# First layer of an equivariant GNN kernel: the dependent half of a chunk is run one chunk later, heads two later and last

## The chip, the cores and the metric

The kernel runs on one core of one Trainium2 chip. The metric is the device time of one execution in microseconds (us), the median of three runs. Nothing is shared with other cores, so there is one span, one TensorE clock and one set of 16 DMA engines to watch.

## The reference, cut to what matters

Two message-passing layers over 3125 nodes and 100000 edges. Each node has 64 scalars and 32 vectors of 3 components. The change touches only the edge loop of the first layer, an attention layer. For every edge that loop computes:

```python
msg = (s_n @ W_src)[src] + (s_n @ W_dst)[dst]          # gathered rows of two node tables, added
w1 = rbf @ W_rbf                                       # edge factors
m1_s, m1_v = _cg_tp(msg_s, msg_v, y0, y1, w1[...])     # products of features, factors and y
a = leaky_relu(m1_s @ W_alpha) * alpha_dot             # attention logits
val_s = m1_s @ Ws_val
val_v = einsum(m1_v, Wv_val) * sigmoid(val_s @ Wg)     # gated values
m2_s, m2_v = _cg_tp(sigmoid(val_s), val_v, y0, y1, w2)
hs, hv = m2_s @ Ws_vlin, einsum(m2_v, Wv_vlin)         # the heads' values, stored per edge
```

## The kernel before, in words

The edges are cut into 392 chunks of 256 (two groups of 128 partitions, G = 2). A chunk passes through five engines in a chain:

- GpSimd (POOL) gathers the rows of `src_tab` and `dst_tab` by four indirect DMAs, six chunks ahead.
- TensorE (PE) makes the factors W1 (`factors0`, L792), ScalarE (ACT) weighs them (`weigh0`, L1111 to L1115).
- VectorE (DVE) adds the gathered rows (`joined0`, L1481) and builds the first mixed tensor M (`products0` to `rest_of_v0`, L1506 to L1532, semaphore `m`).
- PE transposes M (`t1`, L800), ACT copies it out (`copies`, L1126, semaphore `c1`), and PE multiplies it (`e1`, L822 and L824) into the edge bank E1, which holds logits, gates and values.
- DVE takes E1: logits `la` (`gated`, L1543), `svy` (`gated_up`, L1549), `vals` (`summed`, L1556). ACT takes the sigmoids (`squash`, L1137 and L1138, semaphore `sg`). DVE makes V2 (`scaled`, L1574) and the second mixed tensor M2 (`mixed_dots`, `mixed_rest`, L1587 to L1600, semaphore `tp`), ACT its other blocks (`weigh2`, L1149 and L1154, semaphore `m2a`).
- PE transposes M2 (`t2`, also L800), ACT copies it (L1126 again, semaphore `c2`), PE makes the heads in the bank HP (`hm`, L847 and L849, semaphore `h`).
- DVE forms tG and the vector heads (`head_products`, L1610, and `head_values`, L1619, semaphore `hv`), ACT the scalar heads (`scalars0`, L1164, semaphore `hs`), and SP stores the rows (`store`, L507).

Nothing but the code sets the order. Each engine has one in-order list of functions, `stage0(t, total)`, called once for each step t; the number added to t says which chunk the function works on in that step. `loop_steps` writes out the first and last steps and runs the others in a hardware loop of 8 steps, so the loop's branch (L338) comes once in 8 chunks, 47 times in all. Between engines there are only semaphores. Within DVE a second instruction that needs the first one's result waits on DVE's own semaphore `s_dve` (`ch.wait`). `ch.restart` (L81) clears that semaphore at the start of each step.

PE and DVE share three tight resources: E1 has one buffer, HP has one buffer, and M and M2 have two each. A wait such as `pe.wait_ge(LA["hv"], v.num)` in `hm` says that the heads of the chunk before must have been read from HP.

Of the kernel before, what the change touches and what calls it, by code (L numbers as in the profile page):

```python
# [8 lines left out]
ALU = mybir.AluOpType  # L9
# [3 lines left out]
P = 128  # L13
# [4 lines left out]
G = 2  # L18
# [5 lines left out]
C = 32  # L24
# [9 lines left out]
Q = 4  # L34
# [116 lines left out]
def program(nc, a, out):  # L151
    ctx = ExitStack()
    with ctx:
# [6 lines left out]
        def sem(name):  # L160
            return ctx.enter_context(nc.semaphore(name))
# [169 lines left out]
        def loop_steps(eng, q, sups, wide, lead, tail, stage):  # L331


            total = sups * q
            for t in range(-lead, 2 * q):
                stage(Step(t, None, wide, q), total)
            end = sups - 2 - sups % 2
            with eng.Fori(2, end, 2) as base:  # L338
                for u in range(2 * q):
                    stage(Step(u, base, wide, q), None)  # L340
            for t in range(end * q, total + tail):
                stage(Step(t, None, wide, q), total)
# [16 lines left out]
        def inside(v, total):  # L359
# [2 lines left out]

        LA = dict(ix=[sem(f"a_ix{u}") for u in range(2)], rb=[sem(f"a_rb{u}") for u in range(2)],
                  ga=[sem(f"a_ga{u}") for u in range(8)], st=[sem(f"a_st{u}") for u in range(4)],
                  **{k: sem(f"a_{k}") for k in ("w", "ws", "m", "t1", "c1", "e1", "bent", "sg", "vg", "m2a", "tp", "t2", "c2",
                                                "h", "hs", "hv")})

        LM = {k: sem(f"m_{k}") for k in ("ld", "cp", "ab", "mx", "all", "tab", "ix", "ga", "got")}
# [17 lines left out]
        def _(sp):  # L386
# [103 lines left out]
            def load_rbf(v, total):  # L490

                if v.place or not inside(v, total):
                    return
                if v.sup_past(2):
                    sp.wait_ge(LA["w"], v.num - Q)
                sp.dma_start(rbf[0:16, v.sslot].rearrange("f q g p -> f (q g p)"),
                             a["rbf_line"][:, bass.ds(v.data(), 1), :].rearrange("f a e -> f (a e)"))\
                    .then_inc(LA["rb"][v.sslot], 16)

            def store(v, total):  # L500

                if not inside(v, total):
                    return
                sp.wait_ge(LA["hv"], v.num + 1)
                sp.wait_ge(LA["hs"], v.num + 1)
                row = h_tab.ap()[bass.ds(v.column(0), 1), :]
                sp.dma_start(bass.AP(row.tensor, row.offset, [[NC * D, P], [1, G * D]]),  # L507
                             hst[:, v.slot].rearrange("p g f -> p (g f)")).then_inc(LA["st"][v.slot], 16)

            def sp0(t, total):  # L510
                load_places(t + 8, total)
                load_rbf(t + 5, total)
                store(t + -2, total)
            loop_steps(sp, Q, NS, False, 8, 2, sp0)

            def fill(table, width):
                zero = bass.AP(zeros.tensor, zeros.offset, [list(zeros.ap[0]), [0, AR // P], [1, width]])
# [222 lines left out]
        def _(pe):  # L740
# [42 lines left out]
            def factors0(v, total):  # L783

                if not inside(v, total):
                    return
                if v.place == 0:
                    pe.wait_ge(LA["rb"][v.sslot], v.sup_round(16))
                if v.past(1):
                    pe.wait_ge(LA["ws"], v.num)  # L790
                for g in range(G):
                    ins = nc.tensor.matmul(W1[:, 224 * g:224 * (g + 1)], rbf[:, v.sslot, v.place, g, :], w_rbf[:, :],  # L792
                                           start=True, stop=True)
                ins.then_inc(LA["w"], 1)
# [17 lines left out]
            def e1(v, total):  # L812

                if not inside(v, total):
                    return
                pe.wait_ge(LA["c1"], v.num + 1)
                if v.past(1):

                    pe.wait_ge(LA["vg"], v.num)
                    pe.wait_ge(LA["sg"], v.num)  # L820
                for g in range(G):
                    nc.tensor.matmul(E1[:, 0, ES * g:ES * (g + 1)], MT[:, 0, g, :], w_ms0[:, :], start=True, stop=True)  # L822
                    for b in range(2):
                        ins = nc.tensor.matmul(E1[:, 1, P * g:P * (g + 1)], MT[:, 1 + b, g, :], w_mv0[:, b, :],  # L824
                                               start=(b == 0), stop=(b == 1))
                ins.then_inc(LA["e1"], 1)

            def t2(v, total):
                if not inside(v, total):
                    return  # L830

                pe.wait_ge(LA["m2a"], v.num + 1)
                pe.wait_ge(LA["tp"], v.num + 1)
                if v.past(1):
                    pe.wait_ge(LA["c2"], v.num)
                turn(M2[:, v.par], TR2, LA["t2"])
# [15 lines left out]

            def stage0(t, total):
                e1(t + -1, total)
                t2(t + -2, total)
                t1(t, total)
                factors0(t + 2, total)
                hm(t + -2, total)
            loop_steps(pe, Q, NS, False, 2, 2, stage0)

            pe.wait_ge(s_flag, 1)
            general = pe.value_load(flag[0:1, 0:1], min_val=0, max_val=EP)
# [176 lines left out]
        def _(act):  # L1039
# [79 lines left out]
            def copies(v, total, turned, tr, dst, sem_done, freed):  # L1119
                if not inside(v, total):  # L1120
                    return
                act.wait_ge(LA[turned], v.num + 1)

                if v.past(1):
                    act.wait_ge(LA[freed], v.num)
                nc.scalar.activation(dst[:, 0:3].rearrange("p k g e -> p (k g e)"),  # L1126
                                     tr[:, 0:3 * G, :].rearrange("p a e -> p (a e)"), ACT.Copy).then_inc(LA[sem_done], 1)
# [29 lines left out]
            def scalars0(v, total):  # L1157

                if not inside(v, total):
                    return  # L1160
                act.wait_ge(LA["hv"], v.num + 1)
                if v.past(4):
                    act.wait_ge(LA["st"][v.slot], v.slot_round(16, 4) - 16)
                nc.scalar.activation(hst[:, v.slot, :, 0:S], ax(HP[:, 0:1], (S, G), (1, S)), ACT.Copy).then_inc(LA["hs"], 1)  # L1164

            def stage0(t, total):
                weigh0(t + 1, total, 1)
                squash(t + -1, total)
                copies(t + -2, total, "t2", TR2, MT2, "c2", "h")
                copies(t, total, "t1", TR1, MT, "c1", "e1")  # L1170
                weigh2(t + -1, total)
                weigh0(t + 2, total, 0)
                scalars0(t + -2, total)
            loop_steps(act, Q, NS, False, 2, 2, stage0)

            act.wait_ge(s_flag, 1)
            general = act.value_load(flag[0:1, 0:1], min_val=0, max_val=EP)
# [172 lines left out]
        def _(dve):  # L1350
# [201 lines left out]
            def summed(v, total, up):  # L1552

                if inside(v, total):
                    ch.wait(up)
                    return ch.count(TT(vals[:, :, :, :], ax(E1[:, 1, 0:1], (P, G), (C, 3), (1, C)), svy[:, :, :, :], ALU.add))  # L1556

            def bent_sums(v, total):

# [3 lines left out]
                ch.count(nc.vector.tensor_reduce(alog[:, bass.ds(v.column(0), G), :].rearrange("p c h -> p (c h)"),  # L1563
                                                 ax(la[:, 0, 0:1], (LG, G * H), (1, LG)), AX.X, ALU.add))

            def scaled(v, total, summed):

                if not inside(v, total):
                    return
                dve.wait_ge(LA["sg"], v.num + 1)  # L1570
                if v.past(1):
                    dve.wait_ge(LA["m2a"], v.num)
                ch.wait(summed)
                TT(k3(V2[:, :, :]), ax(gate[:, v.par, 0, 0:1], (C, G), (0, 3), (1, C)), vals[:, :, :, :], ALU.mult)\  # L1574
                    .then_inc(LA["vg"], 1)

# [26 lines left out]
            def head_products(v, total):  # L1603

                if not inside(v, total):
                    return
                dve.wait_ge(LA["h"], v.num + 1)
                if v.past(1):
                    dve.wait_ge(LA["hv"], v.num)
                return ch.count(TT(k3(tG[:, :, :]), ax(HP[:, P + 96:P + 97], (P, G), (0, 3), (1, C)), y_of(v, 1, (1, 3), (0, C)), ALU.mult))  # L1610
# [9 lines left out]

            def stage0(t, total):
                ch.restart()
                gated(t + -1, total)
                joined = joined0(t + 1, total)
                ups = gated_up(t + -1, total)
                parts = products0(t + 1, total, joined)
                done = summed(t + -1, total, ups)
                scaled(t + -1, total, done)
                crossed0(t + 1, total, parts)
                dots = mixed_dots(t + -1, total)  # L1630
                bent_sums(t + -1, total)
                mixed_rest(t + -1, total, dots)
                up = head_products(t + -2, total)
                crosses = others0(t + 1, total, parts)
                rest_of_s0(t + 1, total, parts)
                head_values(t + -2, total, up)
                rest_of_v0(t + 1, total, parts, crosses)
            loop_steps(dve, Q, NS, False, 1, 2, stage0)
            ch.restart()


# [314 lines left out]
```

## Time and profile before

| | |
|---|---|
| median of 3 runs | 3868.43 us (3867.98 to 3871.22) |
| the profiled execution, first to last instruction | 4838.8 us |
| edge loop of the first layer | about 85 to 3043 us of that span |
| edge loop of the second layer | about 3448 to 4779 us |
| mean granted TensorE clock | 0.917 of full speed |

The profiled execution is a separate one, and the only time of its own that is known is its span, 970.4 us above the median of the runs. An engine is busy while one of its instructions runs, overlap counted once. "Idle before" an instruction is put down to the semaphore that arrived last; "remote" means that the profile shows no instruction that sent it at that moment. The starts of matmuls are recorded and their ends modelled.

### The profile page before, as it was taken

The numbers are of one execution on the slowest core, as the hardware profiler recorded it, in microseconds if no ns is written. First come the engines' busy times: TensorE is split into PE (matmuls) and PEld (weight loads), VectorE is DVE, ScalarE is ACT, GpSimd is POOL, SyncE is SP. The second block draws the span as 40 slices with busy tenths as digits, with TensorE's granted clock in tenths as the row PEclk, the third lists the DMA queues.
The fourth block names the chain that finished last, engine by engine and source line by source line (L and its number), as shares of the span: only waits on it lengthen the run. The fifth ranks groups of instructions, "written<-read, shape, count | busy, mean of one in ns | idle before, by whom it ended". The sixth has DMA issues, their size and how long they took to land. (4 is left out here: it accounts for less than half of the span.)

```text
span 4838.8 us, 96593 instructions
## 1 busy us (share of the span) xinstructions
PE 3739.1 (77%) x21340; PEld 2828.7 (58%) x21340; DVE 3611.5 (75%) x12738; ACT 3088.6 (64%) x11217; POOL 2474.0 (51%) x2474
## 2 busy tenths in 40 slices
PE   3677777777777777777777778597788888888887
PEld 3676766666676767766666667487433333333334
DVE  4677777777777777777777778788677877777875
ACT  3566666666666666666666667475666666666664
POOL 3445555555555545555555454011366666666663
PEclk7899999999999999999999999799899998998998
DMA  3222222222222222222222222798233333333333
GB/s 101 64 64 68 72 67 68 67 70 67 66 71 72 67 63 72 68 72 67 66 68 68 64 71 63 228 274 226 60 77 77 77 79 76 79 78 77 81 78 103
DMA packets 296922, 411.02 MB, mean 85 GB/s; under 512 B 98580, under 2 KB 231572, under 8 KB 296596
## 3 DMA queue, kind: packets, MB, share of 16 engines
q0 software_dynamic: 127568, 211.04, 19.0%
q1 hardware_dynamic: 169284, 199.21, 12.7%
q8 instruction: 24, 0.39, 0.0%
q14 instruction: 46, 0.38, 0.0%
HBM read 309.09 MB, written 100.94 MB: 85 GB/s over the span
## 5 line engine op out<-in xcount | busy, mean ns | idle before, releaser
L654 POOL DMA_INDIRECT ACC<-src_tab,idx x784 | 777.2, 991 | 1184.8 <-DVE M L1532 852.2
L721 POOL DMA_INDIRECT ACC<-hid_tab,idx x784 | 828.7, 1057 | 453.6 <-issue 250.7
L800 PE MATMUL TR<-ident,M 128*128 128x128 f32 x4704 | 682.7, 285 | 472.0 <-DVE M L1532 380.3
L654 POOL DMA_INDIRECT TAB<-dst_tab,idx x784 | 767.9, 980 | 261.2 <-issue 260.9
L800 PEld LDWEIGHTS TR<-ident,M 128*128 128x128 f32 x4704 | 549.0, 146 | 554.6 <-DVE M L1532 440.0
L1126 ACT ACTIVATE MT<-TR 128x768 f32<-128x768 f32 x784 | 609.5, 842 | 158.2 <-remote 135.7
L1164 ACT ACTIVATE ACC<-HP 128x128 f32<-128x128 f32 x392 | 109.2, 279 | 750.8 <-DVE ACC L1619 625.8
L1115 ACT ACTIVATE ACC<-W,ACC 128x64 f32<-128x64 f32 x2352 | 587.9, 348 | 0.0
L849 PE MATMUL HP<-w_hv,MT 128*128 128x128 f32 x3136 | 564.4, 306 | 0.0
L1309 ACT ACTIVATE ACC<-TR,y 128x128 f32<-128x128 f32 (+1 forms) x1568 | 421.9, 455 | 208.6 <-remote 100.3
L1610 DVE TENSOR_TENSOR tG<-HP,ACC 128x192 f32<-128x192 f32 x392 | 140.1, 357 | 523.1 <-remote 331.3
L824 PE MATMUL E<-w_mv,MT 128*128 128x128 f32 x3136 | 508.3, 288 | 0.0
L824 PEld LDWEIGHTS E<-w_mv,MT 128*128 128x128 f32 x3136 | 471.8, 204 | 0.0
L849 PEld LDWEIGHTS HP<-w_hv,MT 128*128 128x128 f32 x3136 | 453.9, 208 | 0.0
L999 PE MATMUL HP<-M,ohE 128*128 128x480 f32 x800 | 407.9, 636 | 48.8 <-DVE M L1863 29.3
L822 PE MATMUL E<-w_ms,MT 128*128 128x168 f32 x1568 | 383.0, 328 | 68.2 <-ACT MT L1126 62.9
L847 PE MATMUL HP<-w_hs,MT 128*128 128x64 f32 x1568 | 315.0, 286 | 153.4 <-ACT MT L1126 120.5
L999 PE MATMUL E<-M,ohE 128*128 128x480 f32 x768 | 396.6, 643 | 42.5 <-issue 23.3
L792 PE MATMUL W<-w_rbf,rbf 128*128 128x224 f32 x1568 | 405.7, 384 | 27.2 <-DMA rbf<-in_rbf_line 13.8
L847 PEld LDWEIGHTS HP<-w_hs,MT 128*128 128x128 f32 x1568 | 267.1, 208 | 259.3 <-ACT MT L1126 178.7
L1309 ACT ACTIVATE TAB<-TR,y 128x128 f32<-128x128 f32 (+1 forms) x1568 | 415.7, 430 | 0.5 <-PE TR L984 0.5
L984 PEld LDWEIGHTS TR<-w_edge,ACC 64*128 64x128 f32 x1568 | 126.3, 197 | 441.0 <-issue 196.3
(279 smaller groups left out, 8063.1 us busy)
## 6 DMA issues: line engine op xcount, KB each, us to landing
h_tab<-ACC SPq DMA_DIRECT2D x392, 160.0 KB
SC<-h_tab SPq DMA_DIRECT2D x50, 640.0 KB, 4.9
TAB<-h_tab SPq DMA_DIRECT2D x48, 640.0 KB, 5.1
ACC<-in_e64T SPq DMA_DIRECT2D x98, 256.0 KB
ACC<-src_tab,idx POOLq DMA_INDIRECT x784
TAB<-dst_tab,idx POOLq DMA_INDIRECT x784
ACC<-hid_tab,idx POOLq DMA_INDIRECT x784
agg_tab<-ACC POOLq DMA_DIRECT2D x49, 240.0 KB
```

Of the source, the lines that this page charges most:

```text
L654: pool.indirect_dma_start(tile[:, v.slot8, g, :], None, table.ap(), bass.IndirectOffsetOnAxis(ap=idx[:, v.sslot, c:c + 1], axis=0))\
L721: pool.indirect_dma_start(gat1[:, v.slot8, g, :], None, hid_tab.ap(), bass.IndirectOffsetOnAxis(ap=idx[:, v.sslot, c:c + 1], axis=0))\
L792: ins = nc.tensor.matmul(W1[:, 224 * g:224 * (g + 1)], rbf[:, v.sslot, v.place, g, :], w_rbf[:, :], start=True, stop=True)
L800: ins = nc.tensor.transpose(to[:, b * G + g, :], Mt[:, g, lo:lo + w], ident[:, :])
L822: nc.tensor.matmul(E1[:, 0, ES * g:ES * (g + 1)], MT[:, 0, g, :], w_ms0[:, :], start=True, stop=True)
L824: ins = nc.tensor.matmul(E1[:, 1, P * g:P * (g + 1)], MT[:, 1 + b, g, :], w_mv0[:, b, :], start=(b == 0), stop=(b == 1))
L847: nc.tensor.matmul(HP[:, S * g:S * (g + 1)], MT2[:, 0, g, :], w_hs0[:, :], start=True, stop=True)
L849: ins = nc.tensor.matmul(HP[:, P + P * g:P + P * (g + 1)], MT2[:, 1 + b, g, :], w_hv0[:, b, :], start=(b == 0), stop=(b == 1))
L999: ins = nc.tensor.matmul(AG[v.sslot][:, 0:MW], ohE[:, v.slot, g, :], M[:, v.par, g, :], start=(v.place == 0 and g == 0), stop=(v.place == ...
L1115: ins = nc.scalar.activation(o[:, 160 + 64 * k:224 + 64 * k], w[:, 160:224], ACT.Copy, scale=y_at(v, g, 1 + k))
L1126: nc.scalar.activation(dst[:, 0:3].rearrange("p k g e -> p (k g e)"), tr[:, 0:3 * G, :].rearrange("p a e -> p (a e)"), ACT.Copy).then_inc( ...
L1309: ins = nc.scalar.activation(WS[v.slot][:, g, P * k:P * k + hi - lo], wg_[:, lo:hi], ACT.Copy, scale=y1[:, v.sslot, c:c + 1])
```

## The change

Every function keeps its instructions. What changes is the chunk on which it works in a step, its place in the list, and four waits.

- DVE, ACT: everything from `gated` to `mixed_rest` and `squash`, `weigh2` works on chunk t-2 instead of t-1; the copy of the first transposes moves from t to t-1. `weigh0(…, 1)` does its chunk a step earlier.
- PE: `t2` and `hm` work on t-3 instead of t-2; `e1` and `t1` stay. `factors0` runs one chunk further ahead.
- The heads (`head_products`, `head_values`, `scalars0`, `store`) work on t-4 instead of t-2. On DVE both stand last in the step; on ACT the copy of the second transposes stands last.
- A new semaphore `vs` is raised by `summed`. PE's `e1` waits for `vs` and not for `vg`, so E1 is free once `vals` is made. `scaled` waits for `vs` where it waited for `s_dve`.
- `scalars0` waits for `h`, and `head_products` waits for `hs`; before, `scalars0` waited for `hv` and `head_products` for `h`.

```diff
@@ PE
-                    pe.wait_ge(LA["vg"], v.num)
+                    pe.wait_ge(LA["vs"], v.num)
...
                 e1(t + -1, total)
-                t2(t + -2, total)
+                t2(t + -3, total)
                 t1(t, total)
-                factors0(t + 2, total)
-                hm(t + -2, total)
-            loop_steps(pe, Q, NS, False, 2, 2, stage0)
+                factors0(t + 3, total)
+                hm(t + -3, total)
+            loop_steps(pe, Q, NS, False, 3, 3, stage0)
@@ ACT
-                act.wait_ge(LA["hv"], v.num + 1)
+                act.wait_ge(LA["h"], v.num + 1)
...
-                weigh0(t + 1, total, 1)
-                squash(t + -1, total)
-                copies(t + -2, total, "t2", TR2, MT2, "c2", "h")
-                copies(t, total, "t1", TR1, MT, "c1", "e1")
-                weigh2(t + -1, total)
+                squash(t + -2, total)
+                copies(t + -1, total, "t1", TR1, MT, "c1", "e1")
+                weigh2(t + -2, total)
                 weigh0(t + 2, total, 0)
-                scalars0(t + -2, total)
-            loop_steps(act, Q, NS, False, 2, 2, stage0)
+                scalars0(t + -4, total)
+                weigh0(t + 2, total, 1)
+                copies(t + -3, total, "t2", TR2, MT2, "c2", "h")
+            loop_steps(act, Q, NS, False, 2, 4, stage0)
@@ DVE
-                    return ch.count(TT(vals[:, :, :, :], ax(E1[:, 1, 0:1], (P, G), (C, 3), (1, C)), svy[:, :, :, :], ALU.add))
+                    TT(vals[:, :, :, :], ax(E1[:, 1, 0:1], (P, G), (C, 3), (1, C)), svy[:, :, :, :], ALU.add).then_inc(LA["vs"], 1)
...
-                ch.wait(summed)
+                dve.wait_ge(LA["vs"], v.num + 1)
...
-                dve.wait_ge(LA["h"], v.num + 1)
+                dve.wait_ge(LA["hs"], v.num + 1)
...
-                up = head_products(t + -2, total)
                 crosses = others0(t + 1, total, parts)
                 rest_of_s0(t + 1, total, parts)
-                head_values(t + -2, total, up)
                 rest_of_v0(t + 1, total, parts, crosses)
-            loop_steps(dve, Q, NS, False, 1, 2, stage0)
+                up = head_products(t + -4, total)
+                head_values(t + -4, total, up)
+            loop_steps(dve, Q, NS, False, 1, 4, stage0)
@@ SP
-                load_rbf(t + 5, total)
-                store(t + -2, total)
-            loop_steps(sp, Q, NS, False, 8, 2, sp0)
+                load_rbf(t + 6, total)
+                store(t + -4, total)
+            loop_steps(sp, Q, NS, False, 8, 4, sp0)
```

On DVE, the second half of one step of the written-out first steps, with the semaphores that each instruction waits for (`a_h` is `h`, and so on; shapes are partitions by elements):

```order
 L1600 TENSOR_TENSOR M<-fX 128x2x96 [waits s_dve]
-L1610 TENSOR_TENSOR tG<-HP,ACC 128x192 [waits a_hv,a_h]
 L1517 TENSOR_TENSOR fX<-ACC 128x2x2x32
 L1518 TENSOR_TENSOR fX<-ACC 128x2x64
 L1524 TENSOR_TENSOR M<-M 128x2x32 [waits s_dve]
 L1525 TENSOR_TENSOR M<-ACC 128x2x128
-L1619 TENSOR_TENSOR ACC<-HP,tG 128x2x96 [waits s_dve]
 L1531 TENSOR_TENSOR M<-fX 128x2x96 [waits s_dve]
 L1532 TENSOR_TENSOR M<-ACC 128x2x96
+L1610 TENSOR_TENSOR tG<-HP,ACC 128x192 [waits a_hv,a_hs]
+L1619 TENSOR_TENSOR ACC<-HP,tG 128x2x96 [waits s_dve]
 L81 ISA [waits s_dve]
```

Four instructions stood between tG (L1610) and L1619, which needs it; now none does.

On ACT, one step before the change, from the copy L1164 of the scalar heads:

```order
L1164 ACTIVATE ACC<-HP 128x2x64 [waits a_hv]
L1113 ACTIVATE ACC<-W,ACC 128x96
L1115 ACTIVATE ACC<-W,ACC 128x64 x3
L1137 ACTIVATE gate<-E 128x64 [waits a_vg,a_t2,a_bent]
L1138 ACTIVATE M<-E 128x2x2x32
L1126 ACTIVATE MT<-TR 128x768 [waits a_h,a_t2]
L1126 ACTIVATE MT<-TR 128x768 [waits a_e1,a_t1]
L1149 ACTIVATE M<-M,ACC 128x64 [waits a_sg]
```

and the same stretch of a step after it:

```order
L1164 ACTIVATE ACC<-HP 128x2x64 [waits a_h]
L1113 ACTIVATE ACC<-W,ACC 128x96
L1115 ACTIVATE ACC<-W,ACC 128x64 x3
L1126 ACTIVATE MT<-TR 128x768 [waits a_h,a_t2]
L1137 ACTIVATE gate<-E 128x64 [waits a_vg,a_t2,a_bent]
L1138 ACTIVATE M<-E 128x2x2x32
L1126 ACTIVATE MT<-TR 128x768 [waits a_e1,a_t1]
L1149 ACTIVATE M<-M,ACC 128x64 [waits a_sg]
```

The copy of the second transposes (the first L1126 of each) now comes ahead of the sigmoids, and L1164 no longer waits for DVE's heads.

## Rows read from the trace of the kernel before

**Rows 1.** Page, part 1: busy time by engine, whole span

```profile
PE 3739.1 (77%) x21340; PEld 2828.7 (58%) x21340; DVE 3611.5 (75%) x12738; ACT 3088.6 (64%) x11217; POOL 2474.0 (51%) x2474
```

**Rows 2.** Windows: length, busy PE PEld DVE ACT POOL, PE clock, DMA share, GB/s

```profile
0.00:85.00 85.00, 32.86 (x162) 27.52 (x162) 48.74 (x123) 37.03 (x93) 9.30 (x24) 0.83 0.43 116
85.00:3043.00 2958.00, 2252.81 (x15672) 2041.29 (x15672) 2184.80 (x8623) 1918.74 (x7047) 1540.80 (x1564) 0.93 0.25 68
3043.00:3448.00 405.00, 294.36 (x1894) 270.46 (x1894) 311.47 (x424) 241.66 (x774) 51.11 (x60) 0.88 0.78 223
3448.00:4779.00 1331.00, 1119.21 (x3309) 451.37 (x3310) 1046.67 (x3525) 870.54 (x3248) 871.86 (x827) 0.91 0.32 77
...
2998.00:3037.00 39.00, 35.84 (x272) 32.18 (x272) 37.02 (x150) 31.62 (x115) 0.00 (x0) 1.00 0.10 35
```

**Rows 3.** Groups by line, first layer's loop: busy, mean ns | idle before

```profile
L1574 DVE TENSOR_TENSOR V<-gate,vals 128x192 f32<-128x192 f32 x392 | 140.5, 358 | 52.5 <-DVE vals L1556 0.5
...
L1610 DVE TENSOR_TENSOR tG<-HP,ACC 128x192 f32<-128x192 f32 x392 | 140.1, 357 | 523.1 <-remote 331.3 <-PE HP L849 158.0 <-issue 33.2
...
L1543 DVE SCALAR_TENSOR_TENSOR la<-E,adot 128x144 f32<-128x144 f32 x392 | 119.2, 304 | 179.1 <-remote 143.8 <-PE E L824 34.9
```

**Rows 4.** Timeline, mid-loop: start, length, instruction, idle before

```profile
1509.12 0.31 DVE L1543 SCALAR_TENSOR_TENSOR la<-E,adot 128x144 f32<-128x144 f32 x1
...
1509.79 0.32 ACT L1138 ACTIVATE M<-E 128x128 f32<-128x128 f32 x1
...
1510.30 0.34 DVE L1556 TENSOR_TENSOR vals<-E,svy 128x192 f32<-128x192 f32 x1
1510.78 0.36 DVE L1574 TENSOR_TENSOR V<-gate,vals 128x192 f32<-128x192 f32 x1
...
1511.80 0.66 PE L849 MATMUL HP<-w_hv,MT 128*128 128x128 f32 x4
...
1514.24 0.36 DVE L1610 TENSOR_TENSOR tG<-HP,ACC 128x192 f32<-128x192 f32 x1 [1.35 <-remote]
1514.51 0.28 DVE L1517 TENSOR_TENSOR fX<-ACC 128x128 f32<-128x128 f32 x1
```

**Rows 5.** Timeline: the last gather of the first layer's loop

```profile
2995.83 0.95 POOL L654 DMA_INDIRECT TAB<-dst_tab,idx  x1 [0.30 <-issue]
```

**Rows 6.** Timeline after it: one chunk on DVE and PE

```profile
3003.54 0.30 DVE L1543 SCALAR_TENSOR_TENSOR la<-E,adot 128x144 f32<-128x144 f32 x1
3003.68 0.64 PEld L800 LDWEIGHTS TR<-ident,M 128*128 128x128 f32 x6 [0.45 <-DVE M L1532]
...
3005.28 0.30 PEld L847 LDWEIGHTS HP<-w_hs,MT 128*128 128x128 f32 x2 [0.24 <-ACT MT L1126]
...
3006.22 0.66 PE L849 MATMUL HP<-w_hv,MT 128*128 128x128 f32 x4
...
3006.62 0.30 PEld L822 LDWEIGHTS E<-w_ms,MT 128*128 128x128 f32 x2
...
3007.14 0.35 DVE L1610 TENSOR_TENSOR tG<-HP,ACC 128x192 f32<-128x192 f32 x1
...
3008.08 0.69 PEld L800 LDWEIGHTS TR<-ident,M 128*128 128x128 f32 x6
...
3009.08 0.30 DVE L1543 SCALAR_TENSOR_TENSOR la<-E,adot 128x144 f32<-128x144 f32 x1
```

**Rows 7.** Groups by line on POOL, second layer's loop

```profile
L721 POOL DMA_INDIRECT ACC<-hid_tab,idx x779 | 823.8, 1057 | 448.4 <-issue 245.4 <-DVE M L1863 199.3 <-remote 2.7
L694 POOL DMA_DIRECT2D agg_tab<-ACC x48 | 48.5, 1010 | 4.8 <-issue 4.7
```

**Rows 8.** The loop's branch and the semaphore's clearing on DVE's sequencer

```profile
L338 DVEq ALU_OP  x91: 40/40/40, 238.0 to 4695.7; - x91
L338 DVEq COMPARE_BRANCH  x91: 50/56/72, 238.1 to 4695.8; - x91
...
L81 DVEq EVENT_SEMAPHORE_RANGE_CLEAR  x895: 54/54/55, 57.5 to 4777.2; - x179
```

More of the change, by code:

```diff
@@ L364, in program @@
                   ga=[sem(f"a_ga{u}") for u in range(8)], st=[sem(f"a_st{u}") for u in range(4)],
-                  **{k: sem(f"a_{k}") for k in ("w", "ws", "m", "t1", "c1", "e1", "bent", "sg", "vg", "m2a", "tp", "t2", "c2",
+                  **{k: sem(f"a_{k}") for k in ("w", "ws", "m", "t1", "c1", "e1", "bent", "sg", "vs", "vg", "m2a", "tp", "t2", "c2",
                                                 "h", "hs", "hv")})
@@ L1564, in bent_sums, with scaled @@
                                                  ax(la[:, 0, 0:1], (LG, G * H), (1, LG)), AX.X, ALU.add))
-            def scaled(v, total, summed):
+            def scaled(v, total):
                 if not inside(v, total):
@@ L1622, in stage0 @@
                 ch.restart()
-                gated(t + -1, total)
+                gated(t + -2, total)
                 joined = joined0(t + 1, total)
-                ups = gated_up(t + -1, total)
+                ups = gated_up(t + -2, total)
                 parts = products0(t + 1, total, joined)
-                done = summed(t + -1, total, ups)
-                scaled(t + -1, total, done)
+                summed(t + -2, total, ups)
+                scaled(t + -2, total)
                 crossed0(t + 1, total, parts)
-                dots = mixed_dots(t + -1, total)
-                bent_sums(t + -1, total)
-                mixed_rest(t + -1, total, dots)
-                up = head_products(t + -2, total)
+                dots = mixed_dots(t + -2, total)
+                bent_sums(t + -2, total)
+                mixed_rest(t + -2, total, dots)
                 crosses = others0(t + 1, total, parts)
                 rest_of_s0(t + 1, total, parts)
-                head_values(t + -2, total, up)
                 rest_of_v0(t + 1, total, parts, crosses)
-            loop_steps(dve, Q, NS, False, 1, 2, stage0)
+                up = head_products(t + -4, total)
+                head_values(t + -4, total, up)
+            loop_steps(dve, Q, NS, False, 1, 4, stage0)
             ch.restart()
```

## The prediction

> **What bounds the kernel now.** I read the totals first. In the profiled execution VectorE (DVE) is busy 3611.5 us, and no engine is near its span of 4838.8 us [rows 1]. By stretches, the first layer's edge loop takes 2958 us, 7.55 us for each of its 392 chunks, and DVE is busy 2185 us of them, 5.57 a chunk [rows 2]. Then I asked where DVE is idle in that loop. It is idle 523 us ahead of tG (L1610), which waits for the heads from TensorE (PE); 179 us ahead of `la` (L1543), which waits for the edge bank E1; and 52 us ahead of V2 (L1574) [rows 3]. Read so, the change takes away the dearest wait of the kernel, since the heads that DVE reads will have been made a step earlier.
>
> I don't trust that reading, for two reasons.
>
> First, the timed runs. Their median is 3868 us, and the profile shows DVE busy for 3611 of that. All its idle time in a timed run, in both layers, at the start and at the end, is then 257 us at most (if its instructions take as long there), against 1227 us in the profile. So some 970 us of waiting exist only in the profiled execution, and the question is which.
>
> Second, the waits themselves. In the middle of the loop the last matmul of the heads ends by the profile at 1511.80 + 0.66 = 1512.46, and tG starts at 1514.24, 1.78 us later, released by "remote" [rows 4]. The last gather of this loop is issued at 2995.83 [rows 5]. Behind it the same code runs otherwise: the heads' last matmul ends at 3006.88, and tG starts at 3007.14, straight behind the instruction before it. `la` comes at 3003.54 and again at 3009.08, a step of 5.54 us with no wait [rows 6]. From 2998 to 3037, with POOL silent, DVE is busy 37.0 of 39 us [rows 2]. So the chain of waits through PE does fit under DVE's own work. What stretches a step from 5.54 to 7.55 us is that PE's signals arrive late while gathers run.
>
> How much of that lateness is in the timed runs? In the profile it costs (7.55 - 5.54) x 392 = 786 us. The second layer's loop takes 1331/392 = 3.40 us a chunk [rows 2]. POOL needs there two gathers of 1.06 us, each behind an idle 245.4/779 = 0.31 us, and an eighth of an add of 1.01 + 0.3 us: 2.90 us [rows 7]. If that loop falls to this floor in the timed runs, it gives back 0.50 x 392 = 194 us. 786 + 194 = 980 us, and 970 are missing. So I take it that the timed runs have next to none of the lateness, and that the first loop is bound by DVE there at about 5.6 us a step.
>
> **The change, part by part.**
>
> *The waits for tG, `la` and V2.* The gain is what the first loop still waits in a timed run: call it W. By the sum above it is about -10 us, that is 0. Upper bound: let the second layer fall to DVE's own busy time, 1047 us, a return of 284 us; then 786 + 284 - 970 leaves W = 100 us. Let also the stretch between the loops fall from 405 to DVE's 311 us, and W is 194 us. I take 20 us, near the low end, because POOL's row prices the second layer above DVE's.
>
> *tG and L1619 now stand side by side.* L1619 needs tG and waits for it through `s_dve`. Before, four instructions stood between and hid that. The nearest row is V2 behind `vals`: they start at 1510.30 and 1510.78, 0.48 us apart, with `vals` lasting 0.34, so a dependent pair pays 0.14 us from end to start. ACT's sigmoids (1509.79 + 0.32) were long done, so this wait was for `vals` [rows 4]. tG with a successor that needs nothing starts it 0.27 us later (1514.24 to 1514.51). With the dependent pair it is 0.36 + 0.14 = 0.50. Cost 0.22 us a chunk, 0.22 x 392 = 86 us. It is not hidden by anything, since DVE is in order and is the bound. Bounds: 0 if the sequencer handed over at once, 0.22 by the row.
>
> The Trainium skill (VectorE: DVE Perf Modes, section "The DRAIN you can't avoid") says that a semaphore after each copy cost no more than one after the last: "the semaphore costs nothing extra here". By that rule this term would be 0. This trace does not agree: in the 7.55 us steps as in the 5.54 us steps V2 starts 0.48 us behind `vals`, and independent instructions of this size 0.27 us.
>
> *The branch.* Once in 8 chunks, 47 times, DVE's sequencer must wait for tG before it reaches L1619, and only then does it meet the loop's register operation (0.040), branch (0.056) and the clearing of `s_dve` (0.054) [rows 8], a move and two more register operations, and then `la`. L1619 covers 0.27 us of it. Low bound 0 (0.15 us of listed time is under 0.27); high bound six such instructions at 0.14 us each less 0.27, 0.57 us, or 27 us in all. I take the middle, 14 us.
>
> *`vs` for `vg` and `s_dve`.* The wait of V2 stays as it is with another name. E1 is freed at the end of `vals` (1510.30 + 0.34) and not of V2 (1510.78 + 0.36): 0.50 us earlier for PE. PE's step has slack where it isn't late: it waits 0.45 us for M and 0.24 us for the copy [rows 6]. Worth 0 here.
>
> *The heads' new waits.* PE's `hm` for chunk t-3 waits until L1619 has read HP for chunk t-4, and that is now the last instruction of DVE's step. Behind it in PE's queue stand `e1`, `t2`, `t1` and the factors. `hm` takes 1.34 us (3005.28 to 3006.62), `e1` 1.46 (to 3008.08) [rows 6]. So E1 is filled some 3 us into DVE's next step, and `la` of that chunk comes only at the step after. tG waits for ACT's `scalars0`, about 4 us into the step, and stands 5 us into it. Both fit, and I cost them at 0. If the cover goes (PE at half clock, `hm` and `e1` twice as long), PE's round is late before DVE's.
>
> *SP and POOL.* The store waits for the same two heads; the loads of `rbf` keep their distance to `factors0`, since both moved by one. POOL waits for `m`, which DVE raises 0.77 us before its step's end, as before at the same distance of chunks. 0.
>
> *Filling and draining.* Two more steps at the end, nearly empty: between 0 and two steps of 5.54, I take 5 us.
>
> Sum against the median: 3868 + 86 + 14 + 5 - 20 = 3953 us. Against the profiled execution's own span of 4838.8 us it reads otherwise, since there the lateness is real. The step falls from 7.55 to between 5.8 us (5.54 + 0.22 + 0.04) and some 6.3 us, and the span to 4838.8 - 392 x (1.75 to 1.25) = 4150 to 4350 us. I expect a shorter profile and longer timed runs.
>
> **The rivals.**
>
> *The waits are real and the change pays.* For it: every row of idle time. Against it: 3868 us have no room for more than W = 194 us. With that W the time is 3868 + 105 - 194 = 3779 us. It decides from W = 105 us, 0.27 us a chunk. If instead DVE's instructions were all shorter in the timed runs, in the ratio 3868/4839, the gain would be 1.75 x 392 x 0.8 = 549 us: 3320 us. DVE's step of 5.54 us has nothing in it that a quiet PE shortens, so I give the second little. Together 0.18.
>
> *Nothing moves.* W is near 100 us, or the pair tG and L1619 costs little (the skill's rule: 3868 + 14 + 5 - 20 = 3867 us). 3861 to 3876. 0.12.
>
> *PE becomes the bound.* ACT now copies the second transposes last, PE makes the heads last, and `e1` stands behind them. At half clock that round is 0.87 + 2 x 1.34 + 2 x 1.46 + 0.8 + waits, above 7.3 us. The granted clock in this loop is 0.93 [rows 2]; if such steps are one in ten, 39 x 1.5 = 59 us come on top: 4012 us. 0.05.
>
> **How the numbers follow.** A difference under 0.2% (8 us) can't be told from none here. My case, slower by DVE's own step, has 0.65, with its own range of 3880 to 4000: W from 0 to 95, the branch from 0 to 27, the end from 0 to 12. Slower in all 0.70, same 0.12, faster 0.18. The range to hold the time 8 times in 10 is 3820 to 4005, which leaves out most of the faster cases and the half of PE's.
>
> **What would show it.** In the profile after: no idle time ahead of tG, L1619 starting 0.50 us behind tG with 0.14 us idle before it in each chunk (about 52 us of a new idle row at L1619), and a step of 5.76 us behind the last gather in place of 5.54. The span falls while the median rises. I am wrong if that quiet stretch still shows 5.54, if the median falls, or if `hm` or ACT's last copy has DVE waiting at `la` or V2.

## The result and the profile after

The changed kernel takes 3938.2 us (median of four runs, 3936.6 to 3944.2) where the kernel before takes 3868.2 (3866.7 to 3871.2): a ratio of 1.0182, 95% interval 1.0168 to 1.0197. It is slower by 70 us; 3953 us, 85 more than before, was predicted.

Its profiled execution has a span of 3935.9 us and so stands for the timed runs. That of before does not (4838.8 us), so I profiled the unchanged kernel once more, and after is read beside that second profile of before. Page of the kernel after, span and busy time by engine:

```profile
span 3935.9 us, 96689 instructions
PE 3541.6 (90%) x21340; PEld 2675.8 (68%) x21340; DVE 3583.7 (91%) x12738; ACT 3085.8 (78%) x11217; POOL 2638.3 (67%) x2474
```

Page of before, second profile:

```profile
span 3861.1 us, 96593 instructions
PE 3505.3 (91%) x21340; PEld 2635.6 (68%) x21340; DVE 3558.4 (92%) x12738; ACT 3055.0 (79%) x11217; POOL 2488.1 (64%) x2474
```

The kernel before fits in 3861 us with DVE busy 3558 of them, so the 970 us that the first profile has more, and the idle time in [rows 3] that goes with them, belong to that one execution. Windows of after, the first layer's loop, the stretch between, the second layer's loop (columns as in [rows 2]):

```profile
85.00:2380.00 2295.00, 2146.73 (x15673) 1920.63 (x15672) 2168.30 (x8627) 1929.31 (x7049) 1723.78 (x1564) 1.00 0.32 87
2380.00:2790.00 410.00, 299.57 (x1911) 272.60 (x1912) 315.88 (x448) 242.37 (x781) 59.05 (x66) 0.87 0.77 220
2790.00:3875.00 1085.00, 1021.36 (x3292) 416.19 (x3290) 1029.35 (x3496) 856.50 (x3240) 845.43 (x820) 1.00 0.40 94
```

Windows of before, second profile, the same three stretches:

```profile
85.00:2310.00 2225.00, 2110.52 (x15672) 1879.80 (x15672) 2146.80 (x8629) 1895.98 (x7049) 1575.27 (x1564) 1.00 0.34 91
2310.00:2707.00 397.00, 292.67 (x1894) 270.48 (x1894) 304.28 (x420) 240.01 (x772) 51.40 (x60) 0.88 0.78 223
2707.00:3799.00 1092.00, 1028.39 (x3307) 419.31 (x3308) 1036.76 (x3520) 861.49 (x3248) 851.38 (x827) 1.00 0.39 94
```

The bounds of the stretches are read off by eye, but the place is clear: the first layer's loop is some 70 us longer, and the second layer's is not (1085 against 1092). The granted clock there is 1.00 in both, so TensorE's clock has no part in it. Groups by line of after, first loop:

```profile
L1574 DVE TENSOR_TENSOR V<-gate,vals 128x192 f32<-128x192 f32 x392 | 140.5, 358 | 53.2 <-ACT M L1138 1.2
L1619 DVE TENSOR_TENSOR ACC<-HP,tG 128x192 f32<-128x192 f32 x392 | 140.4, 358 | 40.6
L1610 DVE TENSOR_TENSOR tG<-HP,ACC 128x192 f32<-128x192 f32 x392 | 138.0, 352 | 4.5 <-ACT ACC L1164 4.5
L1506 DVE TENSOR_TENSOR M<-ACC 128x192 f32<-128x192 f32 x392 | 136.9, 349 | 0.5 <-DVE svy L1549 0.2
L1543 DVE SCALAR_TENSOR_TENSOR la<-E,adot 128x144 f32<-128x144 f32 x392 | 117.3, 299 | 18.2 <-DVE tG L1610 17.9
```

The same groups of before, second profile, which take the place of [rows 3]:

```profile
L1574 DVE TENSOR_TENSOR V<-gate,vals 128x192 f32<-128x192 f32 x392 | 140.4, 358 | 52.5 <-DVE vals L1556 0.5
L1506 DVE TENSOR_TENSOR M<-ACC 128x192 f32<-128x192 f32 x392 | 139.2, 355 | 15.1 <-ACT ACC L1115 14.6 <-DVE svy L1549 0.2
L1610 DVE TENSOR_TENSOR tG<-HP,ACC 128x192 f32<-128x192 f32 x392 | 135.8, 346 | 2.9 <-PE HP L849 2.7
L1543 DVE SCALAR_TENSOR_TENSOR la<-E,adot 128x144 f32<-128x144 f32 x392 | 115.9, 296 | 0.7 <-PE E L824 0.6
```

Two idle rows are new, 40.6 us ahead of L1619 and 18.2 ahead of `la`; one is gone, 14.6 us at L1506 for ACT's weighing L1115. The idle times at tG and `la`, 523 and 179 us in [rows 3], were 2.9 and 0.7 us. Timeline of after, two places: at the loop's branch, and the end of a step without the branch:

```profile
644.48 0.35 DVE L1610 TENSOR_TENSOR tG<-HP,ACC 128x192 f32<-128x192 f32 x1
644.94 0.36 DVE L1619 TENSOR_TENSOR ACC<-HP,tG 128x192 f32<-128x192 f32 x1
645.68 0.31 DVE L1543 SCALAR_TENSOR_TENSOR la<-E,adot 128x144 f32<-128x144 f32 x1 [0.39 <-DVE tG L1610]
...
1004.13 0.35 DVE L1532 TENSOR_TENSOR M<-ACC 128x192 f32<-128x192 f32 x1
1004.39 0.35 DVE L1610 TENSOR_TENSOR tG<-HP,ACC 128x192 f32<-128x192 f32 x1
1004.85 0.36 DVE L1619 TENSOR_TENSOR ACC<-HP,tG 128x192 f32<-128x192 f32 x1
1005.13 0.30 DVE L1543 SCALAR_TENSOR_TENSOR la<-E,adot 128x144 f32<-128x144 f32 x1
```

L1619 starts 0.46 us behind tG (mean of all 392 steps). Independent neighbours start 0.26 to 0.28 apart (L1532 to tG, L1619 to `la`). The difference is more than the idle time that the group shows (40.6/392 = 0.10 us): two independent instructions overlap by some 0.08 us, and a dependent pair loses that too. At the branch `la` starts 0.74 us behind L1619 in place of 0.28: 0.46 us, once in 8 chunks.

The longer step is DVE's own and not POOL's. Behind the last gather of the loop, with POOL silent, `la` follows `la` by 5.74 us in after, and by 5.54 us in the second profile of before:

```profile
2334.82 0.30 DVE L1543 SCALAR_TENSOR_TENSOR la<-E,adot 128x144 f32<-128x144 f32 x1
2340.56 0.30 DVE L1543 SCALAR_TENSOR_TENSOR la<-E,adot 128x144 f32<-128x144 f32 x1
...
2263.07 0.30 DVE L1543 SCALAR_TENSOR_TENSOR la<-E,adot 128x144 f32<-128x144 f32 x1
2268.61 0.30 DVE L1543 SCALAR_TENSOR_TENSOR la<-E,adot 128x144 f32<-128x144 f32 x1
```

The row of L1506 holds more than its idle time too. In the kernel before it starts 0.27 us behind `svy` (L1549) in six steps of eight, 0.32 in one, and 0.66 in the step behind the branch; in after it is 0.27 throughout. That makes 21 us in 392 chunks. Timeline of before, second profile:

```profile
674.21 0.35 DVE L1549 TENSOR_TENSOR svy<-E,ACC 128x192 f32<-128x192 f32 x1
674.87 0.36 DVE L1506 TENSOR_TENSOR M<-ACC 128x192 f32<-128x192 f32 x1 [0.31 <-ACT ACC L1115]
```

### The profile page after: what moved, and what is told of

The parts are those of the page before. It is cut to its first block and busy times, and to the rows that moved or that the text cites. A ratio compares the mean times of both kernels' runs of the same rounds, so it can differ in the third digit from the quotient of the medians.

```text
span 3935.9 us, 96689 instructions
## 1 busy us (share of the span) xinstructions
PE 3541.6 (90%) x21340; PEld 2675.8 (68%) x21340; DVE 3583.7 (91%) x12738; ACT 3085.8 (78%) x11217; POOL 2638.3 (67%) x2474
## 5 line engine op out<-in xcount | busy, mean ns | idle before, releaser
L654 POOL DMA_INDIRECT ACC<-src_tab,idx x784 | 852.9, 1088 | 339.9 <-issue 230.2
L654 POOL DMA_INDIRECT TAB<-dst_tab,idx x784 | 874.9, 1116 | 250.1 <-issue 248.5
L1126 ACT ACTIVATE MT<-TR 128x768 f32<-128x768 f32 x784 | 663.4, 846 | 5.2 <-PE TR L800 5.2
L1115 ACT ACTIVATE ACC<-W,ACC 128x64 f32<-128x64 f32 x2352 | 580.1, 339 | 0.0
L800 PE MATMUL TR<-ident,M 128*128 128x128 f32 x4704 | 579.5, 273 | 0.0
L849 PE MATMUL HP<-w_hv,MT 128*128 128x128 f32 x3136 | 520.1, 288 | 0.0
L824 PEld LDWEIGHTS E<-w_mv,MT 128*128 128x128 f32 x3136 | 437.5, 192 | 0.0
L849 PEld LDWEIGHTS HP<-w_hv,MT 128*128 128x128 f32 x3136 | 413.2, 192 | 0.0
L822 PE MATMUL E<-w_ms,MT 128*128 128x168 f32 x1568 | 382.8, 326 | 30.3 <-ACT MT L1126 24.6
L792 PEld LDWEIGHTS W<-w_rbf,rbf 128*128 128x128 f32 x1568 | 267.5, 190 | 185.5 <-ACT ACC L1115 170.3
L999 PE MATMUL E<-M,ohE 128*128 128x480 f32 x768 | 358.6, 590 | 15.5 <-DVE M L1863 14.3
L1154 ACT ACTIVATE M<-V,ACC 128x96 f32<-128x96 f32 x784 | 251.0, 367 | 82.2 <-DVE V L1574 78.0
```

Source lines behind the costliest of these rows:

```text
L654: pool.indirect_dma_start(tile[:, v.slot8, g, :], None, table.ap(), bass.IndirectOffsetOnAxis(ap=idx[:, v.sslot, c:c + 1], axis=0))\
L800: ins = nc.tensor.transpose(to[:, b * G + g, :], Mt[:, g, lo:lo + w], ident[:, :])
L849: ins = nc.tensor.matmul(HP[:, P + P * g:P + P * (g + 1)], MT2[:, 1 + b, g, :], w_hv0[:, b, :], start=(b == 0), stop=(b == 1))
L999: ins = nc.tensor.matmul(AG[v.sslot][:, 0:MW], ohE[:, v.slot, g, :], M[:, v.par, g, :], start=(v.place == 0 and g == 0), stop=(v.place == ...
L1115: ins = nc.scalar.activation(o[:, 160 + 64 * k:224 + 64 * k], w[:, 160:224], ACT.Copy, scale=y_at(v, g, 1 + k))
```

## The experiments

The ratios are against runs of the kernel before, made beside each experiment on the same chip. Their medians are 3862.0 to 3863.6 us; beside after it was 3868.2. So where two runs are compared below, each is first set against its own before: after stands 70.0 us above it. The intervals of the ratios are some 5 or 6 us wide to either side. Each run leaves the computation whole.

### The kernel before once more (p0_before_again)

No edit. It asks whether the lateness of [rows 4] is the kernel's or that one execution's.

> The kernel before, unchanged, for a second profile. My theory: the 970 us between its first profile and its timed runs were lateness of TensorE's signals in that one execution, so a second profile has a span near 3867 us, steps of 5.54 to 5.6 us in the first layer's loop, and at most 0.1 us of idle time ahead of tG in each step. Rival: profiling itself makes this kernel late, and the span is near 4839 us again, with 1.3 us idle ahead of tG.

Measured: 3861.2 us, ratio 0.9996 (0.9987 to 1.0005), profiled span 3861.1, the rows above. The lateness belonged to that one execution. The mean step of this loop, `la` to `la`, is 5.630 us in this profile and 5.796 in that of after.

### tG and L1619 apart (e1_pair_split)

```diff
 (after)
+                up = head_products(t + -4, total)
                 rest_of_v0(t + 1, total, parts, crosses)
-                up = head_products(t + -4, total)
                 head_values(t + -4, total, up)
```

> The changed kernel with one line moved: rest_of_v0 (two instructions, 0.53 us) stands between tG and L1619. The chunks, waits and everything else stay as in the changed kernel. My theory (the 70 us are the dependent pair, 0.18 us in 392 steps, and the branch behind its wait, 0.47 us in 47): the step falls back to 5.54 to 5.56 us, also at the branch, and the time to 3938 - 72 - 22 = 3844 us, a little under the kernel before. Rival A (the later heads, last on ACT and PE, made the round through HP and E1 longer): the step stays at 5.74 us and the time at 3938. Rival B (POOL's gathers bound the loop below 5.7 us): about 3868.

Measured: 3845.4 us, ratio 0.9953 (0.9939 to 0.9967), step 5.568. Groups of this run:

```profile
L1619 DVE TENSOR_TENSOR ACC<-HP,tG 128x192 f32<-128x192 f32 x392 | 135.5, 346 | 0.5
L1543 DVE SCALAR_TENSOR_TENSOR la<-E,adot 128x144 f32<-128x144 f32 x392 | 115.5, 295 | 2.4
```

Both new idle rows are all but gone. The run stands 18 us below its own before, so 88 us went with them. All that made the change slower is the place of one call; the rest of the change, with its cost of filling and draining, is a small gain. Neither rival holds: with the heads as late as in after the step is short again, and it isn't stopped at 3868 us.

### The pair kept, but not at the end (e2_pair_before_m)

```diff
 (after)
-                rest_of_v0(t + 1, total, parts, crosses)
                 up = head_products(t + -4, total)
                 head_values(t + -4, total, up)
+                rest_of_v0(t + 1, total, parts, crosses)
```

> The changed kernel with the pair tG, L1619 still side by side, but ahead of rest_of_v0 and so not in front of the branch. My theory: the pair's 0.18 us stays in each of 392 steps and the 0.47 us at the branch goes, 3938 - 22 = 3916 us; M is ready 0.7 us nearer to the step's end than in the changed kernel, which costs nothing. Rival A (round through PE): M and the heads are both late for PE in the next step, 3938 us or above. Rival B (POOL): 3868 to 3890 us.

Measured: 3932.1 us, ratio 1.0181 (1.0167 to 1.0195): 68.5 us above its own before, no better than after, and 16 above the 3916 that I expected. Yet the wait at the branch was gone:

```profile
L1619 DVE TENSOR_TENSOR ACC<-HP,tG 128x192 f32<-128x192 f32 x392 | 140.2, 358 | 41.2 <-DVE tG L1610 0.5
L1543 DVE SCALAR_TENSOR_TENSOR la<-E,adot 128x144 f32<-128x144 f32 x392 | 117.5, 300 | 0.1
...
L1600 DVE TENSOR_TENSOR M<-fX 128x192 f32<-128x192 f32 x392 | 142.9, 364 | 0.0
L1506 DVE TENSOR_TENSOR M<-ACC 128x192 f32<-128x192 f32 x392 | 142.2, 363 | 0.4
L1587 DVE TENSOR_TENSOR M<-V,ACC 128x192 f32<-128x192 f32 x392 | 142.0, 362 | 0.1
```

What took it back was not idle time. Three instructions that the edit does not touch became longer: L1506 has a mean of 363 ns, and 349 in after. All three write M or M2. The edit makes DVE raise `m` later in its step, and `m` is the semaphore that POOL's gathers wait for. So the next run takes only POOL's timing out.

### The same with POOL let loose (e8_e2_pool_free)

```diff
 (e2)
-                if v.past(7):
+                if v.past(8):
-                    wait(LA["m"], v.num - 6)
+                    wait(LA["m"], v.num - 7)
```

> The kernel e2_pair_before_m with POOL's gathers allowed one chunk further ahead (they wait for m of one chunk earlier, which their 8 buffers allow). e2 lost the wait behind the branch and yet had steps of 5.80 us where the changed kernel has 5.74; three DVE instructions (L1506, L1587, L1600) were 25 to 30 ns longer there whenever a gather stood at one certain place. If POOL's place in the step, held there by its wait for m, is what stretches them, freeing POOL moves it and the step falls towards 5.74 us, 3932 - 20 = 3912 us. Rival: the stretch belongs to DVE's order itself, and the time stays at 3932 us within 8.

Measured: 3917.6 us, ratio 1.014 (1.0124 to 1.0156). Groups of this run:

```profile
L1587 DVE TENSOR_TENSOR M<-V,ACC 128x192 f32<-128x192 f32 x392 | 138.0, 352 | 0.1
L1600 DVE TENSOR_TENSOR M<-fX 128x192 f32<-128x192 f32 x392 | 136.7, 349 | 0.0
L1506 DVE TENSOR_TENSOR M<-ACC 128x192 f32<-128x192 f32 x392 | 135.7, 346 | 0.6 <-DVE svy L1549 0.2
L1543 DVE SCALAR_TENSOR_TENSOR la<-E,adot 128x144 f32<-128x144 f32 x392 | 117.6, 300 | 0.1
```

The run stands 55.6 us above its own before. A wait in POOL's queue, of which DVE's idle rows show nothing in this loop, is worth 68.5 - 55.6 = 13 us; the three groups' busy times fall by 4.0 + 6.2 + 6.5 = 16.7. With that out of the way, e8 differs from after in the branch and from e1 in the pair: 70.0 - 55.6 = 14 us for the branch, 55.6 + 18.2 = 74 us for the pair. Both differences still hold a few us of these lengths, and 14 us has 8 us or so of uncertainty to either side. The traces give the branch more: its steps take 6.21 us in after where the others take 5.75, and 5.77 against 5.75 in e8, which is 0.44 to 0.46 us in 47 steps, 21 to 22 us.

### Before with POOL let loose (e9_before_pool_free)

The same two lines, in the kernel before.

> The kernel before with the same looser wait of POOL. Its steps away from the branch average 5.58 us where 5.54 is the shortest. If POOL's place stretches DVE, up to 0.04 us of 392 steps can go: 3863 - 15 = 3848 us. Rival: no change, 3863 us.

Measured: 3855.7 us, ratio 0.998 (0.9971 to 0.9989). A gain of 6.4 us against the 3862.0 beside it, clear of noise but less than half of the 15 that I gave as the most; L1506 falls from 355 to 347 ns:

```profile
L1506 DVE TENSOR_TENSOR M<-ACC 128x192 f32<-128x192 f32 x392 | 136.1, 347 | 15.0 <-ACT ACC L1115 14.5 <-DVE svy L1549 0.2
```

### The heads last, without the shift of chunks (e3_before_heads_last)

```diff
 (before)
-                up = head_products(t + -2, total)
                 crosses = others0(t + 1, total, parts)
                 rest_of_s0(t + 1, total, parts)
-                head_values(t + -2, total, up)
                 rest_of_v0(t + 1, total, parts, crosses)
+                up = head_products(t + -2, total)
+                head_values(t + -2, total, up)
```

> The kernel before with the two lines of the heads moved to the end of DVE's step, side by side; chunks, waits and the other engines' lists are those of before. My theory of the pair: 0.18 us in 392 steps and 0.47 us at 47 branches, 94 us over the kernel before less what it waits for tG there: 3868 + 94 - 25 = 3937 us, if the heads' later reading of HP does not hold TensorE. Rival A (later heads hold TensorE and ScalarE): scalars0 waits for hv and stands ahead of half of weigh0 and of the sigmoids on ScalarE, so each step grows by 0.5 us or more, above 4060 us.

Measured: 4113.0 us, ratio 1.065 (1.0635 to 1.0664), 176 us above my own case. Rival A came true, with the path that it names. Groups of this run:

```profile
L1506 DVE TENSOR_TENSOR M<-ACC 128x192 f32<-128x192 f32 x392 | 143.1, 365 | 127.6 <-ACT ACC L1115 127.4
L1619 DVE TENSOR_TENSOR ACC<-HP,tG 128x192 f32<-128x192 f32 x392 | 140.2, 358 | 40.5
...
L1164 ACT ACTIVATE ACC<-HP 128x128 f32<-128x128 f32 x392 | 108.6, 277 | 558.2 <-DVE ACC L1619 558.2
```

`scalars0` waits for `hv`, which now comes at DVE's step end; ACT stands idle 558 us there, where before has 303, and the weighing behind it makes DVE wait 127 us at L1506. The pair shows the same idle time here as in after (40.5 us). So moving the heads last by itself is dear. After has the heads last without this loss, and ACT's idle time ahead of L1164 is 3.6 us there. It differs in the chunks, in ACT's order and in the waits of the heads, and no run tells which of them is needed.

### Which semaphore frees E1 (e4_vg_frees_bank)

```diff
 (after)
-                    pe.wait_ge(LA["vs"], v.num)
+                    pe.wait_ge(LA["vg"], v.num)
```

> The changed kernel with the edge bank freed by vg again (the end of V2) and not by vs (the end of vals). TensorE's e1 may then start 0.48 us later in each step. My theory: TensorE waits 0.41 us a step for the copy of the second transposes and 0.43 us for the weighed factors in the changed kernel, so it has the slack, DVE stays the bound at 5.74 us, and the time stays at 3938 us within 8. Rival: e1 stands at the head of TensorE's round and hm at its end, the slack is used up, and each step grows by up to 0.3 us, 4050 us.

Measured: 3936.3 us, ratio 1.0187 (1.0173 to 1.02), the same as after, as expected. PE's idle time ahead of `e1` (the weight loads of L822) grows to 219.2 us, where after has 38.6, and nothing follows from it:

```profile
L822 PEld LDWEIGHTS E<-w_ms,MT 128*128 128x128 f32 x1568 | 236.7, 190 | 219.2 <-issue 172.2 <-DVE V L1574 45.0 <-ACT MT L1126 1.9
```

### The other pair taken apart (e6_before_v2_split)

V2 behind `vals` is a pair of the same kind, and has stood in the kernel all along (52.5 us idle at L1574). In the kernel before, `scaled` and `crossed0` change places, as do `bent_sums` and `mixed_dots`:

```diff
 (before)
                 done = summed(t + -1, total, ups)
-                scaled(t + -1, total, done)
                 crossed0(t + 1, total, parts)
-                dots = mixed_dots(t + -1, total)
+                scaled(t + -1, total, done)
                 bent_sums(t + -1, total)
+                dots = mixed_dots(t + -1, total)
```

> The kernel before with two functions of DVE's list swapped: crossed0 (L1512) stands between vals and V2, and bent_sums (L1563) between V2 and mixed_dots. My theory of dependent pairs: the pair vals, V2 costs 0.134 us of idle time and 0.08 us of overlap in each step, so DVE's own step falls from 5.54 to 5.33 us, 84 us in all; how much of it is seen depends on the round through hm and tG, which in this kernel stands just under DVE's step: between 3780 us (all) and 3863 us (none). Rival (a wait on a semaphore costs nothing beyond the finishing of the instruction): no change, 3863 us.

Measured: 3792.1 us, ratio 0.9816 (0.9803 to 0.983), 71 us less than before, of which the row of idle time had shown 52. The rival, in which a wait on a semaphore costs nothing beyond the end of the instruction, has fallen:

```profile
L1574 DVE TENSOR_TENSOR V<-gate,vals 128x192 f32<-128x192 f32 x392 | 140.3, 358 | 0.3
```

### Both pairs apart, in the changed kernel (e7_both_split, e10_both_split_pool_free)

e7 is e1 with the order of e6 (at t-2); e10 is e7 with the two lines of e8.

> The changed kernel with both dependent pairs parted: rest_of_v0 between tG and L1619, crossed0 between vals and V2, bent_sums behind V2. My theory: DVE's own step is 5.33 us, TensorE, ScalarE and the round through HP have 0.4 us of slack at 5.54 us, so 3845 - 84 = 3761 us, below both kernels. Rival A: POOL's four gathers (4 x 1.0 us and 4 x 0.31 us between them, 5.2 to 5.4 us) or ScalarE (5.1 us) come in before DVE: 3780 to 3845 us. Rival B: V2 does not wait for vals but for ScalarE's sigmoids, and then V2's idle time stays: 3845 us.

> The kernel e7_both_split with the same looser wait of POOL. Its steps are 5.38 us against 5.33 us of DVE's own work by the rows. If POOL's gathers (5.2 to 5.4 us a chunk) run close to the bound, more freedom gives 3779 - 20 = 3759 us; if POOL sets no bound and no stretch, 3779 us.

Measured: e7 3779.0 us, ratio 0.978; e10 3776.1 us, ratio 0.9771 (0.9757 to 0.9784). These two are the fastest, and nothing tells them apart: POOL's wait for `m` sets no bound here, and the 20 us that it might have given did not come. e7 is 18 us above the 3761 that I expected, at the edge of Rival A. The gains of e1 (18 us against before) and e6 (71) add up to 89, and e7 has 85: the sum of measured gains holds. Behind the last gather e7's steps take 5.34 us, 0.20 less than before's 5.54 and as good as the 5.33 expected, so DVE's own work was counted rightly. While the gathers run the steps are longer, 5.39 us over the loop, and that part is missing; which disturbance it is stays open. Timeline of e7:

```profile
1002.53 0.34 DVE L1556 TENSOR_TENSOR vals<-E,svy 128x192 f32<-128x192 f32 x1
1002.80 0.28 DVE L1512 TENSOR_TENSOR fX<-ACC 128x128 f32<-128x128 f32 x1
1003.01 0.36 DVE L1574 TENSOR_TENSOR V<-gate,vals 128x192 f32<-128x192 f32 x1
1003.29 0.29 DVE L1563 TENSOR_REDUCE ACC<-la 128x144 f32 x1
```

V2 still starts 0.48 us behind `vals`, as in [rows 4], but an instruction now runs in the gap. The two pairs have the dependence in common and not the bank: tG and L1619 both read HP, while `vals` reads E1 and V2 reads no bank of PE.

## Why the prediction was right

**Which waits are real.** Right, and this step decided it: the timed runs had no room for the idle time of [rows 3], and the second profile shows the loop at 5.63 us a step with DVE busy 2147 of 2225 us. The rival in which the waits are real fell with it. Two conclusions failed. The second layer's loop was priced by POOL at 2.90 us a chunk, and takes 1092/392 = 2.79, so it gave back 239 us and not 194. The sum, 786 + 194 - 970, leaves W at +10 and not at the -10 that the prediction writes, and it was 45 too low by that loop. And "the span falls while the median rises", with 4150 to 4350 us for the profile of after. That took the lateness for a property of every profiled execution. It was one of a single execution; the span after is 3935.9 us. Of the signs named, a step of 5.76 us behind the last gather came as 5.74.

**W, 20 us.** As waits the size was right: 21 us at L1506 by the starts, and next to nothing at tG and `la` (2.9 + 0.7 us of idle time). But the prediction had placed them at tG, `la` and V2. They stand in the step behind the branch, where DVE waits 0.31 us for ACT's L1115. Two edits bear on that wait, `weigh0(…, 1)` a step earlier and L1164 without `hv`, and no run separates them. I had not named it, since [rows 3] gave no sign of it. As the prediction defines W, all of the loop's time above 5.54 us a step, it was more: (5.63 - 5.54) x 392 = 35 us. The rest of it is no wait (see below). To take 20 out of bounds from 0 to 194 was a choice, and that it came so near to 21 is in part luck.

**The pair, 86 us.** Right mechanism, sized a little high. Timeline: 0.46 - 0.27 = 0.19 us a chunk, 74 us; e8 against e1: 74 us. The nearest row, V2 behind `vals`, gave 0.48, of which 0.13 to 0.14 idle, and tG to L1619 is 0.46: 0.10 us idle. (0.50 less 0.27 is 0.23 and not 0.22; it changes the sum by 4 us.) The row expected at 52 us is 40.6. The Trainium skill's sentence "the semaphore costs nothing extra here" (VectorE: DVE Perf Modes, "The DRAIN you can't avoid") is said of a row of copies. It does not carry over to a semaphore on which the next instruction of the same engine waits for its own input: by taking such pairs apart e1 gains 88 us, the branch's share in it, and e6 71.

**The branch, 14 us.** Right mechanism: some 14 us by the timed runs (e8 against after), 22 us by the traces (0.46 us in 47 steps), both inside the bounds of 0 to 27. By the traces it was sized low. The middle of the bounds had no row behind it.

**`vs` for `vg`, the heads' new waits, SP: 0.** Shown for `vs` by e4. tG waits 4.5 us in all for ACT, which is nothing. Whether the new waits are worth anything by themselves no run shows.

**Filling and draining, 5 us.** The first `la` starts 5.3 us later (99.3 against 94.0), and from the last `la` of this loop to the end of the program it is 4.5 us longer: 10 us.

**What the sum lacked.** POOL was put at 0, but the pair behind L1532 also moves `m`, and with it the gathers, to another place in DVE's step. Behind L1506, L1587 and L1600 the next instruction starts 0.03 us a step sooner in after than in before, together 12 us. That the place of the gathers is the cause is inferred: e9 takes 10 us of the same kind out of the kernel before, by POOL's wait alone, but no run tests it on after.

From start to start in the two traces the terms are these: the pair 74 us, L1619 to `la` 25 (22 of them at the branch), L1506 behind `svy` -21, the three groups -12, filling and draining 10. They come to 76 us, where the spans differ by 74.8 and the medians by 70; predicted were 85. The pair was taken 12 us too high and 12 us of shorter instructions were missed, while the branch with the end of the step and the draining were taken 16 us too low. So the mechanism was right, and that the total is only 10 to 15 us off is in part luck, since the errors run against each other.

## What to carry to other kernels

Before the idle rows of a profile are believed, its span is to be set beside the timed median; where they differ by 25%, busy time and a stretch that runs undisturbed say more than any wait. On an engine that sets the pace, two neighbours of which the second needs the first cost 0.19 to 0.21 us more here than neighbours that don't, each time, and the idle row shows only a half to two thirds of it (0.10 and 0.13 us). An independent instruction between them took it back in both places, so look for such pairs (here at V2 and L1619) before waits between engines are moved. Such a pair is dearest directly ahead of a loop's branch (0.46 us more for each branch here), so what ends a loop body should have nothing just ahead of it to wait for. And what moves a semaphore within the step can move another engine: e8 and e9 gained 13 and 6 us by POOL's wait alone, with no idle row of DVE to show it.

## What the runs showed of the hardware that was not expected

- One and the same kernel gave profiled spans of 4838.8 and 3861.1 us. In the first, a signal of PE came 1.78 us late in the middle of the first layer's loop [rows 4], and PE's signals were in time once that loop's gathers had ended [rows 5, 6]; the second layer's loop was 239 us longer too (1331 against 1092). No other profiled execution of this study showed it, so its cause could not be tested and stays open.
- Three of DVE's instructions that write M and M2 (L1506, L1587, L1600) last 343 to 365 ns on the mean of a run. Changing nothing but the wait of the gathers moved L1506 from 363 to 346 ns (e2, e8) and from 355 to 347 (before, e9). By what DVE and POOL disturb each other here was not tested.
